# Gated block with half of its taps on DVE and ACT, its products on GpSimd, eight gate buffers and a new order of each engine

## What is computed

```python
xz = jnp.einsum('blc,dc->bld', x_flat, W_in)            # 64 -> 2 x 128
x_branch, z_branch = jnp.split(xz, 2, axis=-1)
u = jax.lax.conv_general_dilated(x_branch.transpose(0, 2, 1), conv_w, window_strides=(1,),
    padding=[(D_CONV - 1, 0)], feature_group_count=D_INNER, ...)   # 4 causal taps per channel
u = silu((u + conv_b[None, :, None]).transpose(0, 2, 1))
y = (y1 + y2 + y3 + y4) * silu(z_branch)                # the four are all u: 4 u silu(z)
out = jnp.einsum('bld,cd->blc', y, W_out)
```

## Time and profile before

| | before |
|---|---|
| median of 3 runs | 218.71 us (217.41 to 220.54) |
| the profiled execution | 217.4 us, its span 215.5 us |
| PE busy | 203.2 us |
| DVE busy | 154.1 us |
| ACT busy | 138.9 us |
| POOL busy | 94.8 us |
| granted clock of TensorE | 1.00 |
| attention / conv layers / gated block, by PE's timeline | to about 131 / to 176.6 / to 215.5 us |

### The profile page before, as it was taken

One profiled execution on the slowest core, in us unless ns is written; L12 is line 12 of the kernel. 1 busy time (PEld: TensorE's weight loads), 2 busy tenths in 40 slices (PEclk: granted clock), 3 DMA queues, 4 the chain that ended last, 5 costly groups with the idle time before them and its releaser, 6 DMA issues.

```text
span 215.5 us, 6793 instructions
## 1 busy us (share of the span) xinstructions
PE 203.2 (94%) x2734; PEld 143.3 (66%) x2735; DVE 154.1 (71%) x316; ACT 138.9 (64%) x294; POOL 94.8 (44%) x108
## 2 busy tenths in 40 slices
PE   7788999999999999999999998997899999899994
PEld 2356888888888878888788865654566665445441
DVE  4665699977886868878769755999796862625543
ACT  2438598779776987788877762278444364876631
POOL 0349999970325199322792019487435200100000
PEclk9999999999999999999999999999999999999999
DMA  6970000000000000000000000001347700002032
GB/s 211 434 292 0 3 3 6 0 3 5 3 3 3 3 2 3 3 3 3 5 0 3 5 3 0 0 22 24 79 94 171 171 2 0 0 3 75 6 111 106
DMA packets 4701, 10.03 MB, mean 47 GB/s; under 512 B 704, under 2 KB 3520, under 8 KB 4544
## 3 DMA queue, kind: packets, MB, share of 16 engines
q1 hardware_dynamic: 4528, 9.27, 13.6%
q10 hardware_dynamic: 144, 0.34, 0.4%
HBM read 5.03 MB, written 1.61 MB: 31 GB/s over the span
## 4 chain that ended last, share of the span: by engine, by line
PE 75%; ACT 7%; DVE 6%; DMA 4%; POOL 3%; issue 3%; SPq 1%; ACTq 0%; POOLq 0%; DVEq 0%
PE turned L706 12%; PE outs L726 11%; PE scores L695 10%; PE scores L914 5%; PE scores L915 4%; PE qkv L666 4%; PE qkv L676 4%; PE scores L808 4%; PE turned L942 3%; PE scores L823 3%; PE outs L748 2%; PE turned L859 2%; DMA xw<-xw_in 2%; DMA p<-parts 2%; PE scores L932 2%
## 5 line engine op out<-in xcount | busy, mean ns | idle before, releaser
L1035 DVE TENSOR_REDUCE mx<-scores 113x16 f32<-113x784 f32 x32 | 30.9, 965 | 9.5 <-PE scores L695 9.3
L706 PE MATMUL turned<-cst,d 113*113 113x113 f32 x256 | 33.3, 273 | 0.9 <-DVE d L1040 0.9
L706 PEld LDWEIGHTS turned<-cst,d 113*113 113x113 f32 x256 | 27.8, 178 | 8.5 <-issue 7.1
L475 ACT ACTIVATE pt<-turned 113x392 f32<-113x392 f32 x64 | 28.4, 495 | 7.1 <-PE turned L706 5.8
L1040 DVE TENSOR_TENSOR d<-scores,mx 113x784 f32<-113x784 f32 x32 | 31.2, 976 | 1.1
L207 POOL TENSOR_TENSOR kex<-ks,cst 128x784 f32<-128x784 f32 (+1 forms) x16 | 23.2, 1452 | 18.6 <-ACT ks L454 18.5
L726 PEld LDWEIGHTS outs<-vsb,pt 113*49 113x49 f32 x1024 | 26.1, 125 | 6.1 <-issue 2.9
L287 POOL TENSOR_TENSOR rstd<-ve,mhalf 128x1 f32<-128x1 f32 (+1 forms) x15 | 8.7, 578 | 47.5 <-DVE ve L1001 47.3
L445 ACT ACTIVATE scores<-rel 113x784 f32<-113x784 f32 x32 | 26.2, 817 | 5.0 <-DMA rel<-rel_in 3.7
L726 PE MATMUL outs<-vsb,pt 113*49 113x18 f32 x1024 | 29.2, 199 | 0.0
L695 PE MATMUL scores<-kex,qs 32*49 32x196 f32 x512 | 28.2, 332 | 0.0
(11 more groups left out here) (121 smaller groups left out, 365.5 us busy)
## 6 DMA issues: line engine op xcount, KB each, us to landing
p<-parts SPq DMA_DIRECT2D x20, 112.5 KB, 2.3
x<-x_in SPq DMA_DIRECT2D x1, 1568.0 KB, 9.8
out<-res SPq DMA_DIRECT2D x8, 196.0 KB, 1.9
xw<-xw_in SPq DMA_DIRECT2D x2, 392.0 KB, 4.7
xw<-xw_in SPq DMA_DIRECT2D x1, 784.0 KB, 6.6
p<-parts SPq DMA_DIRECT2D x6, 108.8 KB, 2.8
ker<-ker_in SPq DMA_DIRECT2D x2, 288.0 KB, 10.1
late<-late_in SPq DMA_DIRECT2D x1, 417.0 KB, 10.7
```

Of the source, the lines that this page charges most:

```text
L475: act.activation(pt[0:WK, k % 2, j].rearrange("p n (w t) -> p n w t", w=2), ps_t[j][0:WK, :].rearrange("p (n w t) -> p n w t", n=4, w=2)[: ...
L706: mm = pe.transpose(ps_t[j][0:WK, n * P:n * P + WK], d[0:WK, k % 2, h:h + 2, :].rearrange("p a b -> p (a b)")[:, 0:WK], ident[0:WK, 0:WK])
L1035: dve.tensor_reduce(top, sc, AXX, ALU.max).then_inc(max_done, 1)
```

## The change

It touches the gated block almost alone.
- The first half of a group no longer gets its taps from PE. `branch(g)` makes the plain input projection of both images, 395 tokens, in bk[0] and bk[1]; `taps(g)` on DVE multiplies it by the four tap weights (a new column group `taps` of the late weights) into `su`: one product, then six multiply-adds over the two images; ACT makes the first tap of image 1 (`tap`). `gate_u` of these two then applies silu in place. The second half keeps the two 128-row products, now in bk[2] and bk[3].
- `stack_back` writes only the second half (394 columns).
- All z products use bk[6] and bk[7] (before: four banks in turn).
- The products su sz go to POOL, except for the last two, which stay on DVE (`gate_last`); the factor 4 goes into the weights `wo4`. `yy` lies in the memory of `kex`, `res` in that of `xw`.
- `su` and `sz` have eight buffers, `xs` four slots.
- branch(0) and gate_branch(0) stand ahead of conv2 of the last group, and each engine has a new order in this stage; the rsqrt of the last group stands behind the first four products in POOL's.
- The statistics of layer 3 are mixed in bk[4] beyond column 400 (`late_mix`).
- At the head, two fillers instead of six, and DVE writes the key mask ahead of the moments of group 1.

```diff
-        xs = sb("xs", [P, 2, 2, SHF + TOK])
-        su = sb("su", [P, 4, HALF])
-        sz = sb("sz", [P, 4, HALF])
-        yy = sb("yy", [P, 4, HALF])
-        res = sb("res", [P, NG, TOK])
+        xs = sb("xs", [P, NG, 2, SHF + TOK])
+        wo4 = sb("wo4", [P, C])
+        su = sb("su", [P, 8, HALF])
+        sz = sb("sz", [P, 8, HALF])
...
+        res = xw[:].rearrange("p g r t -> p g (r t)")
+        yy = kex[:].rearrange("p a b c -> p (a b c)").rearrange("p (a b) -> p a b", b=HALF)
...
+        late_mix = bk[4][:, 400:512]
...
-            for g in range(NG):
+            for g in range(NG - 1):
                 rsqrt(col(3, g), 1, nth(3, g))
+            for u in range(4 * NG - 2):
+                if u == 4:
+                    rsqrt(col(3, NG - 1), 1, nth(3, NG - 1))
+                v = u // 2
+                pool.wait_ge(su_ready, u + 1)
+                pool.wait_ge(sz_ready, u + 1)
+                if v >= 2:
+                    pool.wait_ge(out_done, v - 1)
+                pool.tensor_tensor(yy[:, u % 4, :], su[:, u % 8], sz[:, u % 8], ALU.mult).then_inc(y_ready, 1)
...
-                act.activation(xs[h, g % 2, w, SHF + 1:SHF + TOK], xflat[q, g, 0:TOK - 1], ACT.Identity,
+                act.activation(xs[h, g, w, SHF - 2 + HALF:SHF + TOK], xflat[q, g, HALF - SHF:TOK - 1], ACT.Identity,
...
+            def tap(g):
+                act.wait_ge(xb_done, g + 1)
+                if g > 1:
+                    act.wait_ge(y_ready, 4 * g - 6)
+                act.activation(su[:, 4 * (g % 2) + 1], bk[1][:, SHF:SHF + HALF], ACT.Identity,
+                               scale=ww("taps")[:, 3:4]).then_inc(first_tap, 1)
             def gate_u(u):
...
+                g, w = u // 4, u % 2
+                if u % 4 < 2:
+                    act.wait_ge(tap_done, 7 * g + 6 + w)
+                    act.activation(su[:, u % 8], su[:, u % 8], ACT.Silu, bias=ww("cb")).then_inc(su_ready, 1)
+                    return
+                act.wait_ge(u_done, 2 * g + w + 1)
+                if u >= 8:
+                    act.wait_ge(y_ready, u - 7)
+                act.activation(su[:, u % 8], bk[2 + w][:, 0:HALF], ACT.Silu, bias=ww("cb")).then_inc(su_ready, 1)
             def gate_z(u):
...
+                act.wait_ge(z_done, u // 2 + 1)
+                if u >= 8:
+                    act.wait_ge(y_ready, u - 7)
+                act.activation(sz[:, u % 8], bk[6 + u % 2][:, 0:HALF], ACT.Silu).then_inc(sz_ready, 1)
...
+                if g == 0:
+                    tap(0)
+                    gate_z(0)
+                    gate_z(1)
+            gate_u(0)
+            gate_u(1)
+            tap(1)
+            for w in range(2):
+                stack_back(2, w)
+            gate_u(2)
+            gate_u(3)
+            gate_z(2)
+            gate_z(3)
+            for w in range(2):
+                stack_back(3, w)
+            for g in range(1, NG):
+                for k in range(4):
+                    gate_u(4 * g + k)
+                if g + 1 < NG:
+                    tap(g + 1)
+                for k in range(4):
+                    gate_z(4 * g + k)
...
-            filler(ps_t[1], 6)
+            filler(ps_t[1], 2)
...
-            conv2(3)
-            mix(col(3, 2), 1, nth(3, 2), ps_qk)
...
+            def branch(g):
+                pe.wait_ge(xs_ready, 2 * g + 2)
+                if g == 0:
+                    pe.wait_ge(x_done, 4 * NG - 2)
                 else:
...
+                    pe.wait_ge(tap_done, 7 * g)
+                for w in range(2):
+                    h = slice(64 * w, 64 * w + 64)
+                    mm = pe.matmul(bk[w][:, 0:HALF + SHF], ww("wx")[h, :], xs[h, g, w, 0:HALF + SHF],
+                                   start=True, stop=True)
+                mm.then_inc(xb_done, 1)
+            def expand(g, w):
+                u = 2 * g + w
+                pe.wait_ge(xs_ready, u + 1)
+                pe.wait_ge(xs_back_ready, u + 1)
+                if g > 0:
+                    pe.wait_ge(su_ready, 4 * g)
+                else:
+                    pe.wait_ge(x_done, 4 * NG)
+                t = xs[:, g, w]
+                pe.matmul(bk[2 + w][:, 0:HALF], g12[:, w, 0], t[:, SHF + HALF:SHF + TOK], start=True, stop=False)
+                pe.matmul(bk[2 + w][:, 0:HALF], g12[:, w, 1], t[:, SHF - 2 + HALF:SHF - 2 + TOK],
                           start=False, stop=True).then_inc(u_done, 1)
             def gate_branch(v):
                 g, a = v // 2, (v % 2) * HALF
                 pe.wait_ge(xs_ready, 2 * g + 2)
...
+                if v > 0:
+                    pe.wait_ge(sz_ready, 2 * v)
                 for w in range(2):
                     h = slice(64 * w, 64 * w + 64)
...
+                    mm = pe.matmul(bk[6 + w][:, 0:HALF], ww("wz")[h, :],
+                                   xs[h, g, w, SHF + a:SHF + a + HALF], start=True, stop=True)
+                mm.then_inc(z_done, 1)
...
+            branch(0)
+            gate_branch(0)
+            conv2(3)
+            mix(col(3, 2), 1, nth(3, 2), late_mix)
+            branch(1)
             for g in range(NG):
...
+                for w in range(2):
+                    expand(g, w)
+                if 0 < g < NG - 1:
+                    branch(g + 1)
+                if g > 0:
+                    gate_branch(2 * g)
+                gate_branch(2 * g + 1)
+                if g == 0:
+                    mix(col(3, 3), 1, nth(3, 3), late_mix)
...
+            dve.wait_ge(ks_ready, 1)
+            mask_keys(dve, 0, 0, 2).then_inc(kex_first, 1)
             dve.wait_ge(ld_x1, 16)
             window_moments(1).then_inc(gn_stats, 1)
-            dve.wait_ge(ks_ready, 1)
-            mask_keys(dve, 0, 0, 2).then_inc(kex_first, 1)
...
+                last = dve.tensor_scalar(wo4[:], ww("wo"), 4.0, None, ALU.mult)
...
+            def taps(g):
+                dve.wait_ge(xb_done, g + 1)
+                if g > 1:
+                    dve.wait_ge(y_ready, 4 * g - 6)
+                n = 7 * g
+                for t in (3, 2, 1, 0):
+                    for w in range(2):
+                        acc, src, k = su[:, 4 * (g % 2) + w], bk[w][:, t:t + HALF], ww("taps")[:, t:t + 1]
+                        if t == 3:
+                            if w == 0:
+                                dve.tensor_scalar(acc, src, k, None, ALU.mult).then_inc(tap_done, 1)
+                                n += 1
+                            else:
+                                dve.wait_ge(first_tap, g + 1)
+                            continue
+                        dve.wait_ge(tap_done, n - (t < 2 or w == 1))
+                        dve.scalar_tensor_tensor(out=acc, in0=src, scalar=k, in1=acc, op0=ALU.mult, op1=ALU.add)\
+                           .then_inc(tap_done, 1)
+                        n += 1
+                return
+            def gate_last(w):
+                u = 4 * NG - 2 + w
+                dve.wait_ge(su_ready, u + 1)
+                dve.wait_ge(sz_ready, u + 1)
+                dve.wait_ge(out_done, 2 * NG - 2)
+                dve.tensor_tensor(yy[:, 2 + w, :], su[:, 6 + w], sz[:, 6 + w], ALU.mult).then_inc(y_last, 1)
...
+            taps(0)
             finish2(3, 0)
...
+            variances(col(3, 2), 1, nth(3, 2), late_mix)
             finish2(3, 1)
             layer_moments(3, 3)
...
+            taps(1)
+            variances(col(3, 3), 1, nth(3, 3), late_mix)
+            stack_front(2, 0)
+            stack_front(2, 1)
+            taps(2)
+            stack_front(3, 0)
+            stack_front(3, 1)
+            result(0)
+            result(1)
+            taps(3)
+            result(2)
+            result(3)
+            result(4)
+            result(5)
+            gate_last(0)
+            gate_last(1)
```

More of the change, by code:

```diff
@@ L42 @@
 for part_ in ((("wq", P), ("wk", P), ("wv", P), ("wp", P), ("bq", 1), ("bk", 1), ("bv", 1), ("bp", 1)),
-              (("b1", 1), ("cb", 1), ("wx", P), ("wz", P), ("cw", 4 * P), ("wo", C))):
+              (("b1", 1), ("cb", 1), ("wx", P), ("wz", P), ("cw", 4 * P), ("wo", C), ("taps", 4))):
     at_ = 0
@@ L186, in program @@
         stacked, thirds_stacked = sems("stacked0 stacked1"), sems("thirds_stacked0 thirds_stacked1")
[L188 to L189 removed]
+        xs_ready, xs_back_ready, xb_done, first_tap, tap_done, u_done, z_done = sems(
+            "xs_ready xs_back_ready xb_done first_tap tap_done u_done z_done")
+        su_ready, sz_ready, y_ready, y_last, out_done, res_ready, stored = sems(
+            "su_ready sz_ready y_ready y_last out_done res_ready stored")
         def pieces(r):
@@ L610, in _ @@
                     stack_back(g, w)
-            for g in range(NG):
-                for gate in (gate_u, gate_z) if g < NG - 1 else (gate_z, gate_u):
-                    for k in range(4):
-                        gate(4 * g + k)
-                if g + 2 < NG:
-                    for w in range(2):
-                        stack_back(g + 2, w)
+                if g == 0:
```

(37 more changed lines are left out.)

67 lines of the change are left out of this document (11 added, 56 removed).

## The result

| | before | after |
|---|---|---|
| median of 20 runs each, side by side | 218.65 us (217.17 to 220.64) | 221.4 us (218.3 to 224.56) |
| ratio, 95% interval | | 1.0103 (1.0075 to 1.013) |
| the profiled execution, its span | 217.4, 215.5 us | 219.98, 217.9 us |
| PE, DVE busy | 203.2, 154.1 us | 198.1, 164.2 us |
| ACT, POOL busy | 138.9, 94.8 us | 138.5, 110.1 us |

The changed kernel is 1.0% slower, where -0.3% was forecast. 221.4 us lies inside the range of 213.5 to 222.0, and the class "within 2%" came true, but the sign was wrong. The ratio leaves out slow runs, nine of the 20 of after among them, each over 1.5% above its fastest, so it is smaller than the quotient of the medians, 1.0126.

What follows compares the result with a forecast made beforehand. The prediction took the last stage as bound by PE at 8.5 us per group. 217.4 - 0.8 (head) + 0.1 (last stage) = 216.7, or 218.0 on the median of 218.7; range 213.5 to 222.0.

Steps and rivals of the forecast that it cites:

- the class "within 2%": Whole kernel: the changed time lies within 2% of before, chance 0.70.
- the replay: Last stage laid out instruction by instruction in each engine's new order; PE idle 1.0 to 8.5 us, net +0.1 us.
- the clock: Last stage: rival that PE's longer gaps lower its clock; no separate size, inside the 0.13 chance of DVE becoming the bound.
- The head: Start of the kernel: fewer fillers and earlier mask start the first scores at about 12.05, -0.8 us passed whole.
- PE's lost work, and the wait of 1.1 us ahead of branch(0): Last stage: net -7.4 us of PE work; PE stands 1.1 us for DVE's finish2(2,1) before branch(0).
- Taps: Last stage on DVE: multiply-adds follow each other every 0.54 us, one taps group 4.0 us, 16 us for four.
- the rival "DVE becomes the bound": Last stage: taps held by POOL's products cost some 0.95 us each, +5.3 us, 223.2 us in all; chance 0.13.
- POOL's product: Last stage: one su sz product on POOL takes 0.85 us, with ends at 0.75 and 1.1.
- DVE and POOL shutting each other out: Last stage: stack_front, variance steps and last two products wait for POOL's products and the reverse, 0.4 us.
- The two waits of 1.2 us ahead of gate_branch(5) and (7): Last stage, groups 2 and 3: PE waits for ACT's sz 8 and 9, then 12 and 13, 1.2 us each.
- PE waiting 2.5 us behind ACT's copies: Last stage: gate_branch(3) waits for sz queued behind ACT's copy of group 3; PE idle from 189.9 to 192.4.
- the median of the runs: Whole kernel: the profiled execution lies 1.3 us below the median of 218.7, so 216.7 becomes 218.0.

Runs made afterwards that it cites:

- experiment 1: The kernel before with the head alone changed (two fillers instead of six, key mask first): 216.64 us, ratio 0.9947 to before.
- experiment 2: The changed kernel with 14 unused filler products in PE's wait ahead of gate_branch(3): 218.54 us, ratio 1.0021 to before.
- experiment 3: The changed kernel with ACT's two copies of group 3 moved behind group 1's sigmoids: 215.85 us, ratio 0.9906 to before.
- experiments 5 and 7: Changed kernel with, in 5, POOL's rsqrt(3,3) ahead of products 2 and 3: 220.65 us; in 7, its 14 POOL products back on DVE: 222.25 us.
- experiment 4: The changed kernel with PE's first contraction of the group before placed between the two gate products: 217.16 us, ratio 0.9943 to before.

## Why the prediction was wrong

Taking the profiled executions, the forecast was a span of 214.8 (215.5 - 0.7) and 217.9 came: 3.1 us more. Times of the replay, which the prediction gives to a tenth, are put 1.0 us earlier below, since conv2(3) began at 172.78 where it had 173.8. At the full clock the sign was already wrong, so two steps failed, and either alone would have turned it: the price of POOL's work (its product, and the shutting out between POOL and DVE), and the clock.

- **The head**: right. -0.8 forecast, 0.9 at mix(3,1), about 1 us in experiment 1 (0.8 at the full clock).
- **PE's lost work, and the wait of 1.1 us ahead of branch(0)**: right, 1.14 for L1220:

```profile
171.25 0.94 PE L945 MATMUL scores<-xs,late 64*128 64x395 f32 x4 [1.14 <-DVE x L1220]
```

- **Taps**: right. Six in 3.29 us, 0.54 apart; POOL doesn't slow them. By the group means of after:

```profile
L1239 DVE SCALAR_TENSOR_TENSOR su<-scores,late,su 128x392 f32<-128x392 f32 x24 | 13.2, 618 | 3.1 <-ACT su L589 2.8
L429 POOL TENSOR_TENSOR kex<-su,sz 128x392 f32<-128x392 f32 x14 | 14.5, 1065 | 17.1 <-ACT sz L609 9.7 <-PE turned L987 7.3
```

That answers the rival "DVE becomes the bound": it did not come. (Its working had a slip: from 0.54 to 0.95 us a tap loses 0.41, not 0.36, 11.5 us for the 28; the forecast itself doesn't rest on it.)

- **POOL's product**: mis-sized, 1.0 us undisturbed and 1.065 in the mean, where 0.85 was taken from a row with a repeated input. The end of the range, 1.1, held it. The Trainium skill's estimate in the prediction (GPSIMD Engine Reference, Engine selection), 1.1 us, was nearer.
- **DVE and POOL shutting each other out**: the first step that failed, right in kind and too small in size; the forecast had 0.4 us for all of it. `stack_front(2)` waited for product 3, as forecast, but then the rsqrt behind the product waited for stack_front in turn: 1.23 in place of 0.55 us, a step the replay did not have. The two products (+0.3, from their size), this (+0.65) and some 0.2 on ACT put sz 4 and 5 back by 1.15 us: gate_branch(3) started at 192.58 for 191.4. PE had come to it on time, 188.93 for 188.9. So the gap was 3.65 us and not 2.5.
- **The two waits of 1.2 us ahead of gate_branch(5) and (7)**: right, 1.08 each. A further 0.3 to 0.4 us is left over at the end of the stage, where the last products of POOL (2.00 for two) and DVE (1.90 for two) also exclude each other; this is a remainder, and no run isolates it.
- **The clock**: the second step that failed, a term put at nothing. The prediction named the rival, put it into the 0.13 of another, and gave it no price: "this stage has the full granted clock (1.00), the upper of the two levels, but with hardly a gap; the longest new gap is 2.4 us". It cost 1.64 us in the profiled execution, and 1.8 by the ratios of experiment 2.

1.15 for the gap, 1.64 for the clock and the remainder are the 3.1 us. At the full clock experiment 2 says it again: +1.0 against before where -0.7 was forecast, so 1.7 us for pace (1.5 by the profile); the rest of the difference of the medians is clock. The prediction also added 1.3 us to its span for "the median of the runs" as if that were noise. It was the ladder, and a change that opens a gap moves the kernel down on it.

The order's part was read rightly and not followed up. The replay itself showed PE waiting 2.5 us behind ACT's copies, a step which nothing needed so early; experiment 3 is that remark made into an edit, worth 2%.

## What to carry to other kernels

When work moves from TensorE to the other engines, the saving comes back as gaps; list them, ask of each whose order makes it, and price the longest at the lower clock too, by rows of the same products. A gap that opens in one place costs more than itself. Take the spread of the kernel before apart by its granted clock before adding it to a forecast: two rungs 1.3 us apart are a mechanism, and a change can move a kernel up or down on them. An earlier start on one engine shortens a wait only if the engine that waits does not start earlier by the same cause.

## What the runs showed of the hardware

- TensorE's granted clock fell after waits of 3.65, 3.52 and 3.99 us in the profiled executions of after and of experiments 5 and 7, to means of 0.88 and 0.78, 0.63 and 0.69, and 0.77 and 0.55 in the two stretches of 5 us from 190 on. It held after 2.84 us in experiment 4. After the other gap it fell in two profiled executions (waits of 2.12 and 1.95 us, experiments 4 and 7) and held in the others, and after 1.08 it fell in none. Like waits gave unlike falls, so one execution does not price it; a ladder of runs does.
- Products without use, 3.2 us of them, kept the clock up in the profiled execution (1.00) and made a kernel 1.8 us faster.
- The shutting out of DVE and POOL works both ways. A pair of `stack_front` takes 1.36 to 1.40 us alone, 2.18 behind a POOL product and 2.69 beside four; an rsqrt step of 0.55 us takes 1.21 to 1.28 beside stack_front. The multiply-adds that read PSUM ran beside POOL's products at 0.54 us each, undisturbed. The Trainium skill (GPSIMD Engine Reference, Specifications) names contention with DVE instructions that have two SBUF inputs or run in a two-port mode. The traces agree in that the taps, one of whose inputs is in PSUM, were not held; stack_front has one SBUF input, so only the two-port mode could be its case, and no trace shows an instruction's mode. The pair alone, in after:

```profile
172.34 1.36 DVE L1258 TENSOR_SCALAR xs<-x,rstd,nmr 64x784 f32<-64x784 f32 x2
```
